# Two-layer graph network with a 16-expert feed-forward: seven dense and nine gathered experts instead of eight and eight, a router product of its own, an earlier plan, full w3 tiles

## What is computed

```python
def _swiglu(x, w1, w2, w3):
    a = x @ w1
    return a * jax.nn.sigmoid(a) * (x @ w2) @ w3
gate_out = x @ gate_w + routing_bias
top_v, top_i = jax.lax.top_k(gate_out, 4)
chosen = jax.nn.one_hot(top_i, 16, dtype=x.dtype).sum(axis=-2)
probs = jax.nn.softmax(jnp.where(chosen > 0, gate_out, NEG), axis=-1)
weights = probs * chosen
out = _swiglu(x, sw1, sw2, sw3)                      # shared
for e in range(16):
    out = out + _swiglu(x, w1[e], w2[e], w3[e]) * weights[..., e:e + 1]
```

## Time and profile before

| what | value |
|---|---|
| median of 3 runs | 500.94 us (499.9 to 1226.36) |
| profiled execution, its span | 500.3 us |
| PE busy | 483.9 us (97%) |
| DVE / ACT busy | 272.4 us (54%) / 205.5 us (41%) |
| loads | 191 MB, mean 382 GB/s, 16 DMA engines' share 96.0% |
| granted PE clock, mean | 0.990 |

### The profile page before, as it was taken

The page is one execution under the profiler, slowest core; times in us unless marked ns, Lnnn a source line. Parts: engine busy times, 40 slices in busy tenths (PEclk is TensorE's granted clock), DMA queues, the critical chain, the costliest instruction groups (busy, mean ns, idle before and its releaser), DMA issues.

```text
span 500.3 us, 6706 instructions
## 1 busy us (share of the span) xinstructions
PE 483.9 (97%) x2596; PEld 309.9 (62%) x2596; DVE 272.4 (54%) x326; ACT 205.5 (41%) x227; POOL 9.1 (2%) x46
## 2 busy tenths in 40 slices
PE   8989799999999999999999999999999999999987
PEld 4755433447887666576666756656666676565554
DVE  6734530146889674466538357546555645753542
ACT  1110101035787264555435345455444535545320
POOL 2000000010100000000000000000000000000000
PEclk9989999999999899999999999999999999999999
DMA  8999999999986989999999999999999999999980
GB/s 335 422 420 421 423 419 420 417 419 409 414 357 232 374 279 351 412 417 400 373 417 416 356 417 415 374 404 417 415 364 415 416 363 417 415 398 373 418 327 23
DMA packets 37555, 191.05 MB, mean 382 GB/s; under 512 B 4218, under 2 KB 4602, under 8 KB 32148
## 3 DMA queue, kind: packets, MB, share of 16 engines
q1 hardware_dynamic: 37328, 190.48, 96.0%
q10 hardware_dynamic: 196, 0.14, 0.1%
HBM read 190.35 MB, written 0.26 MB: 381 GB/s over the span
## 4 chain that ended last, share of the span: by engine, by line
PE 84%; DMA 6%; DVE 6%; ACT 2%; issue 2%; POOL 0%; SPq 0%; ACTq 0%; DVEq 0%; POOLq 0%
PE ps L1712 15%; PE ps L1783 13%; PE ps L1726 13%; PE ps L1796 7%; PE ps L1716 7%; DMA w_raw<-in_w 6%; PE ps L1360 4%; PE ps L1524 3%; PE ps L1763 2%; PE ps L1553 2%; PE ps L1541 1%; PE ps L1353 1%; PE ps L1422 1%; PE ps L1438 1%; DVE s_lo L981 1%
## 5 line engine op out<-in xcount | busy, mean ns | idle before, releaser
L967 DVE TENSOR_TENSOR s_lo<-w_raw,s_hi 128x1365 fp32r<-128x1365 f32 x72 | 111.9, 1579 | 69.4 <-ACT s_hi L710 68.4
L710 ACT CAST s_hi<-w_raw 128x1365 fp32r<-128x1365 f32 x72 | 94.4, 1333 | 49.6 <-DMA w_raw<-in_w 48.1
L1712 PE MATMUL ps<-s_hi,xT_hi 128*128 128x512 f32 (+2 forms) x216 | 86.2, 399 | 2.1 <-DVE s_lo L967 2.1
L1712 PE MATMUL ps<-s_lo,xT_hi 128*128 128x512 f32 (+2 forms) x216 | 80.0, 372 | 0.0
L1726 PE MATMUL ps<-w_raw,exS 128*64 128x512 f32 x480 | 74.2, 455 | 0.0
L723 ACT CAST s_hi<-w_raw 128x1536 fp32r<-128x1536 f32 (+1 forms) x36 | 48.9, 1369 | 52.5 <-DMA w_raw<-in_w 51.8
L981 DVE TENSOR_TENSOR s_lo<-w_raw,s_hi 128x1536 fp32r<-128x1536 f32 (+1 forms) x36 | 57.7, 1619 | 2.3 <-ACT s_hi L723 2.0
L1726 PEld LDWEIGHTS ps<-w_raw,exS 128*64 128x64 f32 x480 | 33.2, 136 | 40.0 <-issue 40.0
L1716 PE MATMUL ps<-s_hi,xT_lo 128*128 128x512 f32 (+2 forms) x216 | 57.0, 372 | 0.0
L1712 PEld LDWEIGHTS ps<-s_hi,xT_hi 128*128 128x128 f32 x216 | 41.0, 190 | 21.4 <-issue 11.8
L1712 PEld LDWEIGHTS ps<-s_lo,xT_hi 128*128 128x128 f32 x216 | 41.1, 190 | 8.3 <-issue 1.9
(11 more groups left out here) (296 smaller groups left out, 449.0 us busy)
## 6 DMA issues: line engine op xcount, KB each, us to landing
w_raw<-in_w SPq DMA_DIRECT2D x128, 682.5 KB, 12.0
w_set<-in_w SPq DMA_DIRECT2D x31, 1024.0 KB, 24.6
w_raw<-in_w SPq DMA_DIRECT2D x27, 768.0 KB, 11.8
w_raw<-in_w3s SPq DMA_DIRECT2D x24, 768.0 KB, 12.1
w_raw<-in_sw SPq DMA_DIRECT2D x8, 682.5 KB, 15.7
w_raw<-in_w SPq DMA_DIRECT2D x9, 512.0 KB, 12.2
wk_sb<-in_wk SPq DMA_DIRECT2D x2, 1024.0 KB, 16.8
wq_sb<-in_wq SPq DMA_DIRECT2D x2, 1024.0 KB, 16.0
```

What stands on the lines that cost most here:

```text
L710: a.copy(s_hi[pair_of(g)][:, 0:F1], raw[:, 0:F1]).then_inc(hi_ready, 1)
L967: v.tensor_tensor(s_lo[pair][:, 0:F1], raw[:, 0:F1], s_hi[pair][:, 0:F1].bitcast(F32), ALU.subtract).then_inc(lo_ready, 1)
L1712: mm(bank(i + c0 // D)[:, 0:n], xT_hi[:, k], w[:, c0:c0 + n], start=(k == 0 and w is hi), stop=False)
```

## The change

- The kinds become `"D" + "SD" * 7 + "SS"`. All 16 routed experts are sorted: seven dense, nine gathered. m = 1 is no longer routed expert 0 but the fullest of the nine gathered ones, so SP waits for `table` before the first load of m = 1.
- w3 of a gathered expert is laid out in 11 full tiles: five for each half, and one that holds the last 44 rows of both halves on partitions 0 to 43 and 64 to 107. `CW` is 684. The load to 48 partitions is gone; the last down product is one for all 128 columns. DVE writes the two tails of h by two operations more (`gated_tails`).
- The router is a product of its own (`route`) behind w1 unit 0 of m = 0, with `gate_hi`, `gate_lo`.
- The plan runs during m = 0. Its small tensors have experts on 16 partitions, and PE does the sums and lookups (`count_chosen`, `place_experts`, `place_positions`, `turn_gates`, `place_gates`). DVE does `router_max`, `choose` and `plan_order` before `lo_w2(0, 0)`, and waits for rstd before `lo_w1(0, 3)`. ACT does xn and the exponential between the second and third high part of w2.
- The first gathered expert is gathered alone in m = 0 (`gather_first`), the other eight in four rounds in m = 1, with the spreads in m = 1's down product.

The core of the diff:

```diff
-KINDS = "DD" + "SD" * 7 + "S"
+KINDS = "D" + "SD" * BUSY + "SS"
...
-            next_up(1, 0, w1[0])
-            next_up(1, 1, w2[0])
-            for u in range(W3_UNITS):
-                wait_unused(0, 2, u)
-                load_down(w3[1], u)
             sp.wait_ge(table_ready, 1)
-            for m in range(2, NE):
+            for m in range(1, NE):
...
-            lo_w1(0, 3)
             dve.wait_ge(squares_ready, 1)
             v.tensor_scalar(var_eps[:], x3_squares, LN_EPS, None, ALU.add).then_inc(var_ready, 1)
+            dve.wait_ge(rstd_ready, 4)
+            lo_w1(0, 3)
...
+            def plan_order():
+
+                dve.wait_ge(plan_ps, COUNTED)
+                v.scalar_tensor_tensor(order_col[:], counts_col, float(E1), expert_no[0:E1], ALU.mult, ALU.subtract)
+                then(v.scalar_tensor_tensor(order_row[:], counts_row, float(E1), iota[0:E1, 0:E1], ALU.mult, ALU.subtract))
+                then(v.tensor_scalar(ahead[:], order_row[:], order_col[:], None, ALU.is_gt))
+                then(v.tensor_reduce(place_no[:], ahead[:], AX_X, ALU.add))
+                v.tensor_scalar(at_place[:], iota[0:E1, 0:E1], place_no[:], None, ALU.is_equal).then_inc(plan_ready, 1)
+                then(v.tensor_copy(chosenT[:], chosenT_ps))
+                v.scalar_tensor_tensor(positionT[:], beforeT_ps, 1.0, chosenT[:], ALU.add, ALU.mult).then_inc(plan_ready, 1)
+                dve.wait_ge(plan_ps, PLACED)
+                v.tensor_copy(table[0:1], placed_ps).then_inc(table_ready, 1)
...
+            router_max()
+            choose()
+            plan_order()
             lo_w2(0, 0)
             lo_w2(0, 1)
+            plan_tokens()
             lo_w2(0, 2)
             lo_w2(0, 3)
-            router_max()
+            routed_gates()
+            v.memset(hS[:, S_OWN], 0.0)
+            lo_w3(0, 0)
             gated(0)
+            turned_gates()
+            lo_w3(0, 1)
+            plan_gates()
...
+            def route():
+
+                for k in range(KT):
+                    mm(gate1_out, xT_hi[:, k], gate_hi[:, k], start=(k == 0), stop=False)
+                    mm(gate1_out, xT_hi[:, k], gate_lo[:, k], start=False, stop=False)
+                    last = mm(gate1_out, xT_lo[:, k], gate_hi[:, k], start=False, stop=(k == KT - 1))
...
+            def first_expert():
+
+                up_part(0, 0, 0)
+                route()
+                up_part(0, 0, 1)
+                up_with_hi(unit_w1(0, 2), 0, 2)
+                count_chosen()
+                up_with_lo(unit_w1(0, 2), 0, 2)
+                up_with_hi(unit_w1(0, 3), 0, 3)
+                place_experts()
+                place_positions()
+                up_with_lo(unit_w1(0, 3), 0, 3)
+                up_part(0, 1, 0)
+                up_part(0, 1, 1)
+                up_with_hi(unit_w2(0, 2), NC, 2)
+                gather_first()
+                up_with_lo(unit_w2(0, 2), NC, 2)
+                up_part(0, 1, 3)
+                turn_gates()
```

More of the change, by code:

```diff
@@ L420, in few_no, with own_rows @@
         return SPARSE.index(m)
-    def down_loads(m, u):
-        return 16 * sum(2 if not is_full(i) and u == W3_UNITS - 1 else 1 for i in range(m + 1))
+    def own_rows(g):
+        return slice(FEW * g, FEW * g + FEW)
     block = nc.Block()
@@ L521, in next_down @@
             def next_down(m, e):
+                w = one_down(w3, e + 1) if is_full(m) else one_down(w3s, e)
                 for u in range(W3_UNITS):
[L523 to L530, removed]
+                    wait_unused(m - 1, 2, u)
+                    load_down(w, u)
             sp.wait_ge(unit_ps, 2)
@@ L1213, in routed_gates @@
                 then(v.reciprocal(small[:, 7:8], small[:, 6:7]))
[L1214 to L1230, removed]
-                then(v.tensor_tensor(scratch[:], at_place[:], iota[:, 0:E1].unsqueeze(1).to_broadcast(places), ALU.mult))
-                then(v.tensor_reduce(expert_at[:], scratch[:], AX_X, ALU.add))
-                v.tensor_copy(table[:], expert_at[:]).then_inc(table_ready, 1)
@@ new lines, in place_experts, with place_positions, turn_gates @@
+            def place_experts():
+                pe.wait_ge(plan_ready, ORDERED)
+                mm(placed_ps, expert_no[0:E1], at_place[:], start=True, stop=True).then_inc(plan_ps, 1)
+            def place_positions():
+                pe.wait_ge(plan_ready, POSITIONS)
+                mm(position_at, positionT[:], at_place[:, BUSY:E1], start=True, stop=True).then_inc(plan_ps, 1)
+            def turn_gates():
+                pe.wait_ge(plan_ready, PLAIN)
+                mm(plainT_ps, plain[:], ident[:], start=True, stop=True).then_inc(plan_ps, 1)
@@ new lines, in place_gates, with gather_first @@
+            def place_gates():
+                pe.wait_ge(plan_ready, PLAIN_T)
+                mm(gate_at, plainT[:], at_place[:], start=True, stop=True).then_inc(plan_ps, 1)
+            def gather_first():
+                pe.wait_ge(rows_ready, 1)
+                pe.wait_ge(hots_ready, 1)
+                pe.wait_ge(xn_ready, 7)
+                for k in range(KT):
+                    last = mm(first_gathered[:, FEW * k:FEW * k + FEW], xn[:, P * k:P * k + P], hots[:, 0], start=True, stop=True)
+                last.then_inc(round_ps, 1)
@@ L1876, in _ @@
                             pe.wait_ge(hTS_ready, len(S_HT) * few_no(last_e) + t // KT + 1)
[L1877 to L1878 removed]
+                    own = own_rows(g) if t < S_OWN else slice(0, P)
+                    last = mm(last_halves[b][own], hTS[:, t, own], w3_raw[:, i, HALF[b]], start=(t == 0), stop=(t == S_OWN),
                               skip_group_check=True)
```

340 lines of the change are left out of this document (183 added, 157 removed).

## The result

| | before | after |
|---|---|---|
| median of the runs beside each other | 500.42 us (4 runs) | 492.32 us (4 runs, 491.33 to 493.42) |
| ratio after / before | | 0.9848, 95% interval 0.9822 to 0.9873 |
| profiled execution, its span | 500.3 us | 491.3 us (time of that run 493.42) |
| PE busy | 483.9 us (97%) | 478.7 us (97%) |
| DVE / ACT busy | 272.4 / 205.5 us | 251.3 / 190.4 us |

A forecast was written before the change was run, and what follows sets the result against it. DMA was taken as slightly slower than PE before (about 42 against 41.16 us a pair), with PE leading after. 176.0 + 155.9 + 132.2 + 16.7 + 11.3 = 492.1 us span, 0.6 more for the median: 492.7, likeliest 490 to 495 (0.57).

The forecast's parts named there:

- What bounds: Steady state: 48-partition load slows DMA to about 42 us a pair; full tiles give 40.7, below PE's 41.16.
- m = 0: First expert block, holding nearly all new cost: its end was forecast at 151.1 us.
- The first stall: In m = 0, PE at count_chosen waits for DVE's choose, delayed by rstd: 0.8 us (0.2 to 1.5).
- The second stall: In m = 0, PE waits for w2's low part, behind DVE's wait for placed_ps: 1.3 us (0 to 3).
- The queue: Loads from m = 1 wait for table; first w1 tile lands at 146.2, wanted at 151.1: hidden by 4.9 us.
- m = 1: Second expert, now gathered: 18.89 us block plus four gathers, place_gates and nine spreads, 24.9 us, ending at 176.0.
- Pairs: Dense plus gathered block after m = 1: PE work per block unchanged, 41.16 us a pair.
- The end: Last gathered block behind another gathered expert, 16.7 us, then the closing tail with gated tails, 11.3 us.
- A: Rival: new stalls in m = 0 cause one or two clock drops, handovers 1 us longer: 495 to 498 us; chance 0.18.
- C: Rival: PE falls to 1.2 GHz at the first stall for the rest of m = 0: 503 us; chance 0.06.
- Rival B: Steady state: dip has another cause and stays, DMA bounds at 42.2 us a pair: 494 to 495 us; chance 0.07.
- D: Rival: no stalls at the start (-2.1 us) and cheaper thin products: 489 to 490 us; chance 0.12.

The follow-up runs named there:

- the two splits: Changed kernel, last 512 KB of each gathered w3 as two loads: by partition halves 509.44 us; by tile on all 128 partitions 491.41 us.
- lo_before_table: Changed kernel, DVE writing the low part of w2 unit 0 before it waits for the expert places: 490.60 us, ratio 0.9802.
- after_again: The changed kernel timed once more, nothing altered, as base of a later group: 491.27 us, ratio 0.9812 to the kernel before.

## Why the prediction came out, step by step

**What bounds.** Right. The dip was the load to 48 partitions: it goes when that load goes, comes back with it, and the two splits show that the partitions make it. Without it DMA (40.7 us a pair) is behind PE, and the extra PE work counts in full. The margin is small: PE's pair is 40.92 us, so by these two figures (an estimate) PE can get only some 0.2 us a pair faster before the queue binds again.

**m = 0.** From the first w1 product it took 151.26 - 131.29 = 19.97 us; forecast were 151.1 - 129.36 = 21.7. The failed terms are the small ones:
- The first stall (0.8) did not come. I took POOL's power at 1.81 us, and it took 0.55. In the trace of before the same instruction had taken 0.55 at 48.80 and at 107.72 us, so one row was too little to go by. DVE's `choose` began at 135.27 and ended at 137.27; PE wanted it at 137.75:

```profile
132.59 0.55 POOL L597 TENSOR_TENSOR rstd<-var_eps,neg_half 128x1 f32<-128x1 f32 x1 [10.80 <-DVE var_eps L1161]
```

- The second stall (1.3) was 0.61. It is where I had put it, DVE waiting for the places with the low part of w2 behind it, and `lo_before_table` took it away:

```profile
140.61 0.16 DVE L1232 CAST table<-ps 1x16 int32<-1x16 f32 x1 [0.74 <-PE ps L1843]
140.70 3.05 DVE L973 TENSOR_TENSOR s_lo<-w_raw,s_hi 128x1365 fp32r<-128x1365 f32 x2
```

- `route` took 1.24 us and not 1.5 (134.55 is its end), `count_chosen` 0.64 and not 1.1. For the latter I misread: from 148.19 to 148.33 lie two instructions, not one, so eight come to about 0.6.

These four terms come to 2.2 us, but m = 0 was only 1.8 shorter. The units behind the small products and the stall took longer than the 1.25 us for six products that I had (134.55: 1.34, 142.32: 1.51), and I had no term for that.

**The queue.** Right in its cover, and right in its clock time by luck. First load issued at 141.78 (forecast: about 142):

```profile
141.78 18.53 SPq L503 DMA_DIRECT2D w_raw<-in_w  x12
```

Counted from the first w1 product that is 10.5 us, and I had some 12.8: the table came 2 us sooner, and the part began 1.9 us later. What counts is the cover. m = 1 wanted the tile sooner too, and 3.8 us later costs nothing while 8.4 us later costs a wait of 3.06 us, so the cover is 8.4 - 3.1 = 5.3 us; I had 4.9.

**m = 1.** 176.80 - 151.26 = 25.5 us against 24.9. Three of the four gather rounds take 1.05 to 1.06, where I took 0.86 from the earlier trace rows: 0.6 us. The old stall of 2.07 us and the slow clock behind it are gone.

**Pairs.** PE's work per pair was said to be unchanged. That step was wrong by 0.24 us: w2 unit 0 behind the last down product is 0.2 shorter, the down product 0.05 longer, and the rest is in hundredths. From m = 2 to the last block it came to 463.32 - 176.80 = 286.5 us, where 155.9 + 132.2 = 288.1 were forecast: 1.6 us.

**The end.** From the last pair, which ends at 458.57 + 4.75 = 463.32, to 491.3 are 28.0 us; forecast were 16.7 + 11.3 = 28.0.

**The sum.** The part came to 360.0 against 362.7: -1.8 in m = 0, +0.6 in m = 1, -1.6 in the pairs (together -2.7 before rounding). Two terms outside went the other way. The part began 1.9 us later in the profiled run than before. At 35 to 40 and 50 to 55 us the clock was at 0.50 and 0.66, where before had 0.70 and 0.83 (and 0.83 at 45 to 50, where after had 1.00):

```profile
35.00:40.00 5.00, 5.00 (x24) 5.00 (x25) 0.85 (x2) 0.00 (x0) 0.00 (x0) 0.50 1.02 424
50.00:55.00 5.00, 4.34 (x16) 2.51 (x14) 0.70 (x2) 0.59 (x1) 0.55 (x1) 0.66 1.02 423
```

The one other changed kernel of these profiles with such a late start (131.2, the one with more PE work) shows the same low stretch in its slices; those with a start at 129.1 to 129.7 don't. Before had a milder fall at 35 to 40 and lost little by it at 129 us. At 58.78 us its chain is 2.0 us behind that of `after_again` (56.75), which kept the clock at 35 to 40, yet its experts start only 0.2 us later. The chain of `after_again` shows what covers it: it runs for 24 us through a load that lands at 110.09.

```profile
86.09 24.00 DMA wv_sb<-in_wv
```

The first profile of after is 4.1 us behind at that place (60.89), and like that of before its chain has no such wait; 2.15 us are left at the start of the experts. And the time is 2.1 us above the span of its own run, where I took 0.6 by comparing a median with the span of another run. In the kernel before, the two are 1.7 apart when taken from one run (500.94 and 499.2), and 1.7 to 1.8 in each of its runs in the three groups; in the changed kernel they are 2.1 to 2.2 apart. So 0.3 us of the change's cost lie outside the span; the full tiles alone have 1.7 to 1.8, so it came with kinds and plan. Errors of -2.7, +1.9 and +1.5 make up the 0.7 us between 492.7 and 493.4; the median is 0.4 under the forecast. It is closer than its terms deserve.

**The rivals.** A and C needed a clock that falls in m = 0; the granted clock is 1.00 there. Their mechanism is real all the same: 3.06 us of idle PE were followed by 5.6 us at 0.50. Rival B was undersized: with the dips left in, I expected 494 to 495 and the old loads gave 497.2, 6.0 us above the changed kernel beside them. It had no term for the longer pairs. D was half right: the second stall was halved and the first absent, but the clock at 35 to 55 us took it back in the first runs.

## What to carry to other kernels

When PE and the DMA queue are within 2% of each other, look for the window in which the bytes fall while the DMA share stays at 1.0, and give that load all 128 partitions, even if some bytes more are moved. A chain of small handovers put under large products costs little if the waiting engine has a large operation to do before each wait; look at what stands in its order directly behind the wait. Price an operation from all of its rows in the trace, not from one (POOL's power had two at 0.55 us and one at 1.81). Take the time and the span of one and the same run, and compare a part of the kernel from a mark inside it, not from zero.

## What the runs showed of the hardware

- A load of 512 KB in two halves of the partitions cost 2.9 us of the queue (417 to 242 and 347 GB/s over 10 us), the same bytes by tiles on 128 partitions nothing (418 and 414). The 192 KB on 48 partitions had cost 1.5 us in the window of the earlier trace rows, and 1.8 with the window ahead of it, which moved 394 GB/s.
- The first unit of six products behind a group of half-wide products took 1.44 us; where the group's last product is full-width it took 1.24. The shorter time comes with the full tiles alone (first row) and goes with the old loads in the changed kernel (second row). No run changed the last product by itself, and it isn't the whole rule: at 174.44 of before such a unit took 1.48 behind a full-width gather.

```profile
211.50 1.24 PE ps L1715 x6
188.49 1.44 PE ps L1719 x6
```

- POOL's power on 128 x 1 took 1.81 us at 131.85 of before and as much in the full tiles alone, and 0.55 in every kernel with the new plan and earlier in before, by the trace. Why isn't settled.
- PE idle for 3.06 us was followed by 5.6 us at the lower level (0.50), which cost about 2.8 us more, as the 2.07 us before and the 2.06 us of the full tiles alone were followed by 0.73 and 0.76 in 165 to 170, and 2.45 us of the split by partition by 0.68. 1.98 us near the end of before, and 1.93 and 1.95 us of the split by partition, were not. Before, behind the 1.98 us:

```profile
476.80:482.00 5.20, 5.20 (x23) 4.28 (x24) 3.62 (x4) 1.49 (x3) 0.00 (x0) 1.00 1.01 411
```

- The clock between 30 and 55 us falls by different amounts in executions of one kernel, and with it moves the span, by up to 2 us (489.1 to 491.3 for the changed kernel); the experts' part stayed at 360.0 in each profile.
